# A graph network on one core: x copied into the first hop's table behind the table of places, by ScalarE, and no dense rounds beside the gathers of x

## What is computed

```
h = x
for k in 1..5:                       # layer 0: two such convolutions, 64 -> 128 -> 64
    msg = h[row] * norm[:, None]     # norm = dis[row] * edge_weight * dis[col]
    h   = segment_sum(msg, col, num_segments=100000)
    out = out + h @ W[k]
...
agg = segment_sum(x[src], dst) / count     # layer 1: means of neighbours, then attention of 4 heads
h   = agg @ W_sl + b_sl + x @ W_sr         # layers 2 and 3: such a mean, and attention again
```

## Time and profile before

| | us |
|---|---|
| timed runs, median of 3 | 11474.29 |
| lowest and highest of them | 11440.55, 11497.55 |
| profiled execution, first to last instruction (span) | 11533.1 |
| first gather of x | 18.5 |
| last gather of x | 875.8 |
| first gather of the first hop | 908.9 |

### The profile page before, as it was taken

One profiled execution on the slowest core, in us unless ns is written; L12 is line 12 of the kernel. 1 busy time (PEld: TensorE's weight loads), 2 busy tenths in 40 slices (PEclk: granted clock), 3 DMA queues, 4 the chain that ended last, 5 costly groups with the idle time before them and its releaser, 6 DMA issues. The chain is left out here.

```text
span 11533.1 us, 77998 instructions
## 1 busy us (share of the span) xinstructions
PE 6012.4 (52%) x19953; PEld 3133.7 (27%) x19953; DVE 5136.8 (45%) x14393; ACT 3452.3 (30%) x6468; POOL 6426.5 (56%) x6274
## 2 busy tenths in 40 slices
PE   1453545455454894535454440039778795530287
PEld 1442222222222442212122220013322463320154
DVE  1122333333333554445445446843434894440475
ACT  0002434334241332323233330013333573210143
POOL 6425556566555546556665666756555004657466
PEclk7556767777676996767677675559889897765698
DMA  5243322222223772222222222222233452222243
GB/s 155 55 61 89 89 73 88 79 74 80 66 85 103 214 215 77 79 64 82 76 77 85 65 75 65 76 56 63 65 62 63 138 187 69 65 56 51 78 136 109
DMA packets 1086306, 1021.95 MB, mean 89 GB/s; under 512 B 653551, under 2 KB 709245, under 8 KB 1073313
## 3 DMA queue, kind: packets, MB, share of 16 engines
q1 hardware_dynamic: 847422, 884.62, 24.7%
q0 software_dynamic: 200480, 130.29, 6.4%
q10 hardware_dynamic: 37955, 2.05, 0.4%
HBM read 494.44 MB, written 599.31 MB: 95 GB/s over the span
## 5 line engine op out<-in xcount | busy, mean ns | idle before, releaser
L762 POOL DMA_INDIRECT gathered<-u,place_of_source x1564 | 1625.6, 1039 | 955.9 <-issue 467.5
L762 POOL DMA_INDIRECT gathered<-hop,place_of_source x1564 | 1590.1, 1017 | 1015.5 <-DVE weighted L797 502.4
L811 DVE SCALAR_TENSOR_TENSOR sums<-sums,same_as_before,weighted 128x64 f32<-128x64 f32 x3510 | 987.3, 281 | 263.6 <-remote 109.8
L762 POOL DMA_INDIRECT gathered<-x,row_of_source x782 | 809.8, 1036 | 506.9 <-issue 245.1
L824 DVE SCALAR_TENSOR_TENSOR first_node_sum<-sums,ends_first,first_node_sum 128x64 f32<-128x64 f32 x2786 | 775.5, 278 | 136.2 <-remote 78.4
L695 DVE SCALAR_TENSOR_TENSOR dense_a<-dense_a 128x512 f32<-128x512 f32 x98 | 67.9, 693 | 1590.4 <-ACT dense_b L675 1251.2
L525 PE MATMUL bank<-dense_a,bd_gmean 128*128 128x512 f32 x196 | 195.9, 1102 | 939.3 <-ACT dense_out L516 581.9
L525 PE MATMUL bank<-dense_tmp,mean 128*128 128x512 f32 x980 | 553.5, 681 | 228.7 <-ACT dense_tmp L534 109.0
L762 POOL DMA_INDIRECT gathered<-in_x_dram,dst_index x392 | 393.1, 1003 | 470.6 <-DMA xc<-gathered 348.1
L2651 POOL DMA_INDIRECT out_dram<-lane_out,node_to_write x392 | 398.5, 1017 | 333.3 <-ACT lane_out L2570 224.1
L762 POOL DMA_INDIRECT gathered<-y,place_of_source x391 | 403.9, 1033 | 317.9 <-issue 116.0
(11 more groups left out here) (530 smaller groups left out, 14927.1 us busy)
## 6 DMA issues: line engine op xcount, KB each, us to landing
head_sums<-head_sums SPq DMA_DIRECT2D x98, 1024.0 KB
y<-conv_out SPq DMA_DIRECT2D x294, 256.0 KB
conv_out<-y SPq DMA_DIRECT2D x245, 256.0 KB
hop<-sums SPq DMA_DIRECT2D x196, 256.0 KB
turned<-rows_turned SPq DMA_DIRECT2D x196, 256.0 KB
cat<-turned SPq DMA_DIRECT2D x196, 256.0 KB
u<-conv_out SPq DMA_DIRECT2D x196, 256.0 KB
lane_raw<-x SPq DMA_DIRECT2D x196, 256.0 KB
```

What stands on the lines that cost most here:

```text
L762: return e.indirect_dma_start(out=into, out_offset=None, in_=tab, in_offset=bass.IndirectOffsetOnAxis(ap=index, axis=0), bounds_check=top, ...
L811: e.scalar_tensor_tensor(s[:, k, :], b, go[:, t:t + 1], m[:, k, :], ALU.mult, ALU.add).then_inc(st.summed.handle, 1)
```

## The change

- The copy of x leaves SP's list. ScalarE issues it: `x_in` for three blocks ahead of its part of the table, three more behind it, and then in a loop `x_out(b)` and `x_in(b + 4)` for all 98 blocks. There are `XB` = 6 buffers, three of them new, in `cat[1]`, which is free behind the table.
- All blocks get their places in the buffer before they are stored; `table_store` is gone, and so are the fills with "no place". Each store waits for its `table_place`.
- `weights_vector` becomes a list of steps. VectorE takes a step or so of it behind each `table_place`; the spreads of weights are issued at block 40 and waited for at block 50.
- The 16 groups of x gathers have no dense rounds any more: `EARLY` is 16, the slots of the hops share 16 rounds a lane, and those of the ups have one more round a lane than before.

The diff, cut to its core:

```diff
@@ -208,6 +208,7 @@
...
         SPREADS = 2 * (2 + 2 + 4)
+        SPREAD_BY = 50
...
@@ -338,23 +339,30 @@
...
         def weights_vector(e):
+            yield 0
...
             e.memset(t_m[:], 0.0).then_inc(chain.handle, 1)
+            yield 2
...
             e.memset(s_lin[:], 0.0).then_inc(chain.handle, 1)
+            yield 5
...
             e.tensor_copy(t_w3T[:].rearrange("p h d -> p (h d)"), PS[0][0:D, 0:W4]).then_inc(chain.handle, 1)
...
             e.tensor_copy(s_c, PS[3][0:D, 0:1]).then_inc(chain.handle, 1)
+            yield 12
...
             e.tensor_tensor(s_c, s_c, t_bb[0:D, 1:2], ALU.add).then_inc(chain.handle, 1)
+            yield SPREAD_BY
...
             e.tensor_reduce(t_v[:], t_bg[:], AX.X, ALU.add).then_inc(chain.handle, 1)
+            yield SPREAD_BY + 1
...
@@ -369,31 +377,41 @@
...
             e.tensor_tensor(wts["center"][:], wts["center"][:], ident[:], ALU.add).then_inc(chain.handle, 1)
+            yield SPREAD_BY + 2
...
             for i, w in enumerate(squares):
+                yield SPREAD_BY + 3 + 2 * i
...
                 e.tensor_copy(turned[:], PS[0][:, 0:P]).then_inc(chain.handle, 1)
...
             e.tensor_reduce(wts["v_lin"][0:2 * HEADS, :], t_b4[:, 0, :], AX.X, ALU.add).then_inc(chain.handle, 1)
+            yield SPREAD_BY + 29
...
             e.tensor_scalar(wts["v_lin"][0:2 * HEADS, :], wts["v_lin"][0:2 * HEADS, :], 0.2, None, ALU.mult).then_inc(chain.handle, 1)
+            yield 1 << 20
...
@@ -628,7 +646,7 @@
...
         if lo == 0:
-            yield W.n(0, 0)
+            yield -DENSE_STEPS
...
@@ -1006,7 +1024,10 @@
...
             xs = [a[:].rearrange("p k s d -> p (k s d)")[:, 0:K8 * XW].rearrange("p (k d) -> p k d", d=XW) for a in both]
+            XB = 6
             cat = [sb(ctx, f"cat{i}", [P, 2, 2, 512]) for i in range(2)]
+            xs += [cat[1][:].rearrange("p m a n -> p (m a n)")[:, i * K8 * XW:(i + 1) * K8 * XW].rearrange("p (k d) -> p k d", d=XW)
+                   for i in range(XB - len(both))]
...
@@ -1068,8 +1089,8 @@
...
             xc_got = [sem(f"xc_gathered{i}", 16 * K8 * n) for i, n in enumerate(in_slots(RING, lambda g: 1))]
-            xs_in = [sem(f"x_in{i}", 16 * len(range(i, DB, 3))) for i in range(3)]
-            xs_out = [sem(f"x_out{i}", 16 * len(range(i, DB, 3))) for i in range(3)]
+            xs_in = [sem(f"x_in{i}" if i < 3 else f"own_loaded{i - 3}", 16 * len(range(i, DB, XB))) for i in range(XB)]
+            xs_out = [sem(f"x_out{i}" if i < 3 else f"sums_stored{i - 3}", 16 * len(range(i, DB, XB))) for i in range(XB)]
...
@@ -1093,17 +1114,13 @@
...
             APART = DENSE_STEPS / DENSE_LANES
-            EARLY = 17
-            FREE = 16
-            PER_GROUP = 2
+            EARLY = 16
...
             LOADS_PER_GROUP = 6
-            STORES_PER_GROUP = 3
-            FREE_SHARE = 0.5
-            LATER = PER_GROUP * (NG - FREE)
-            placed_x = sem("shares_in_bank", DB - LATER)
+            SPREAD_AT, LINEAR_AT = 40, DB
+            placed_x = sem("shares_in_bank", DB)
             BUSY = NG - RING
-            SLOTS = len(hops) * BUSY + FREE_SHARE * FREE
+            SLOTS = len(hops) * BUSY
...
@@ -1112,8 +1129,7 @@
...
             def early(slot):
-                slots = FREE_SHARE * min(slot + 1, FREE) + busy_slots(slot + 1 - FREE)
-                return slots / SLOTS * (EARLY * DENSE_STEPS + 2 * APART)
+                return busy_slots(slot + 1) / SLOTS * (EARLY * DENSE_STEPS + 2 * APART)
...
@@ -1305,18 +1321,25 @@
...
 
-            def table_store(e, blocks):
-                e.wait_ge(*tv(6))
-                for b in blocks:
-                    at, n = node_rows(b)
-                    e.wait_ge(*xs_out[b % 3](16 * (b // 3 + 1)))
-                    e.dma_start(x66_rows[at:at + n * K8, 0:2].rearrange("(p k) v -> p k v", k=K8), table[0:n, b, :, :]
-                                ).then_inc(table_put.handle, 16)
+            def x_in(e, b):
+                i = b % XB
+                at, n = node_rows(b)
+                e.wait_ge(*xs_out[i](16 * (b // XB)))
+                e.dma_start(xs[i][0:n, :, 2:XW], x[at:at + n * K8, :].rearrange("(p k) d -> p k d", k=K8)
+                            ).then_inc(xs_in[i].handle, 16)
+            def x_out(e, b):
+                i = b % XB
+                at, n = node_rows(b)
+                e.wait_ge(*xs_in[i](16 * (b // XB + 1)))
+                e.wait_ge(*placed_x(b + 1))
+                e.dma_start(x66_rows[at:at + n * K8, :].rearrange("(p k) d -> p k d", k=K8), xs[i][0:n, :, :]
+                            ).then_inc(xs_out[i].handle, 16)
...
             def table_place(e, b):
-                i = b % 3
+                i = b % XB
                 n = node_rows(b)[1]
-                e.wait_ge(*xs_out[i](16 * (b // 3)))
+                e.wait_ge(*xs_out[i](16 * (b // XB)))
...
@@ -1491,9 +1514,8 @@
...
                     xc_gpsimd(e)
-                    e.wait_ge(*table_put(16 * LATER))
-                    for i in range(3):
-                        e.wait_ge(*xs_out[i](16 * len(range(i, DB, 3))))
+                    for i in range(XB):
+                        e.wait_ge(*xs_out[i](16 * len(range(i, DB, XB))))
...
@@ -1531,39 +1553,14 @@
...
 
-                    def x_in(b):
-                        i = b % 3
-                        at, n = node_rows(b)
-                        e.wait_ge(*xs_out[i](16 * (b // 3)))
-                        e.dma_start(xs[i][0:n, :, 2:XW], x[at:at + n * K8, :].rearrange("(p k) d -> p k d", k=K8)
-                                    ).then_inc(xs_in[i].handle, 16)
-                    def x_out(b):
-                        i = b % 3
-                        at, n = node_rows(b)
-                        e.wait_ge(*xs_in[i](16 * (b // 3 + 1)))
-                        if b >= LATER:
-                            e.wait_ge(*placed_x(b - LATER + 1))
-                        e.dma_start(x66_rows[at:at + n * K8, :].rearrange("(p k) d -> p k d", k=K8), xs[i][0:n, :, :]
-                                    ).then_inc(xs_out[i].handle, 16)
                     steps = early_steps(dense_sync, e)
-                    x_in(0)
                     for g in range(NG):
-                        for b in range(PER_GROUP * g, PER_GROUP * (g + 1)):
-                            if b + 1 < DB:
-                                x_in(b + 1)
-                            x_out(b)
...
                         deque(islice(weight_loads, LOADS_PER_GROUP), 0)
-                        if g > NG - FREE:
-                            table_store(e, range(LATER // 2 + STORES_PER_GROUP * (g - (NG - FREE) - 1),
-                                                 min(LATER, LATER // 2 + STORES_PER_GROUP * (g - (NG - FREE)))))
...
                         e.dma_start(columns(xc, g), flat(ring[i]).rearrange("p (k d) -> p k d", d=D)).then_inc(xc_put[i].handle, 16)
-                        steps.to(early(g - (NG - FREE) - 1))
                     deque(weight_loads, 0)
+                    steps.to(0)
...
@@ -1571,7 +1568,7 @@
...
                                 rows_keep(e, n, g - 2)
-                            steps.to(early(FREE + n * NG + g - 1))
+                            steps.to(early(n * NG + g - 1))
...
@@ -1656,13 +1653,11 @@
...
                     steps = early_steps(dense_tensor, e)
-                    for g in range(FREE):
-                        steps.to(early(g))
...
                                 hop_turn(e, st, n, g - 2)
-                            steps.to(early(FREE + n * NG + g - 0.2))
+                            steps.to(early(n * NG + g - 0.2))
...
@@ -1691,20 +1686,25 @@
...
                     planes_scalar(e)
+                    for b in range(len(both)):
+                        x_in(e, b)
                     table_scalar(e)
-                    weights_spread(e)
-                    table_store(e, range(0, LATER // 3))
+                    for b in range(len(both), XB):
+                        x_in(e, b)
+                    for b in range(DB):
+                        if b == SPREAD_AT:
+                            weights_spread(e)
+                        x_out(e, b)
+                        if b >= 2 and b + XB - 2 < DB:
+                            x_in(e, b + XB - 2)
                     weights_spread_linear(e)
-                    table_store(e, range(LATER // 3, LATER // 2))
...
                     steps = early_steps(dense_scalar, e)
-                    for g in range(FREE):
-                        steps.to(early(g))
...
                                 rows_move(e, n, g - 2)
-                            steps.to(early(FREE + n * NG + g))
+                            steps.to(early(n * NG + g))
...
@@ -1731,9 +1731,6 @@
...
                     e.memset(early_sum[0][:], 0.0)
-                    for i in range(3):
-                        e.memset(xs[i][:, :, 0].bitcast(I32), ABSENT)
-                        e.memset(xs[i][:, :, 1], 0.0)
...
@@ -1843,23 +1840,21 @@
...
```

(23 more changed lines are left out.)

3 lines of the change are left out of this document (added).

## The result

The changed kernel takes **11583.99 us** (median of 4 runs, 11533.68 to 11609.08), the kernel before in the same comparison 11485.92: **1.0078** of it, 95% interval 1.0046 to 1.0111. It is slower by 0.8%, some 53 to 127 us. The forecast was 11283, faster.

A forecast was written before the change was run, and what follows sets the result against it. The head was taken as bound by the table of places, late through a TensorE stall blamed on copies of x, then by the remaining copy. First hop -246, dense +50, hop start +5: -191 from 11474 gives 11283 us; range 11175 to 11570.

The forecast's parts named there:

- Copies out of the table's way: Head: without copies of x beside it, TensorE keeps its pace and the table is done at 410, 285 us earlier.
- My two counter-examples: TensorE at full pace beside gathers at 94.7 and after 909, taken as evidence that gathers alone don't cause the stall.
- SP stores xc without copies in between, so GpSimd ends near 535: Gathers of x: GpSimd no longer waits behind SP, and its end is covered by the copy.
- The copy behind the table: After the table: 98 blocks at 2.4 us, 235 us, plus 5 to fill and 10 for 16 spreads of weights.
- third rival: Copy crawls: the stall moves with the copies, 3.6 us a block, first hop at 766, 11386 us; chance 0.14.
- Dense rounds moved: Hops and ups: moving 45 steps a lane out of the gathers of x costs +50 us, between 25 and 108.
- Start of the first hop: First hop: TensorE may still be slow right behind the copies; +5 us, between 0 and 15.
- Nothing like it shows: First hop: after 909 the present trace was said to show no slow TensorE, so only 5 us were added.
- The second: Rival: the stall comes from gathers or something else that stays; table still at 695, 11560 us, slower; chance 0.08.
- The first rival: The stall belongs to the profiled execution alone; timed runs lack it, the change gives 11568 us, slower; chance 0.17.

The follow-up runs named there:

- pause_33: Changed kernel, but GpSimd waits for the table of places ahead of its group 33 of gathers of x; 1.0006 of the kernel before.
- pause_39: Changed kernel, but GpSimd waits for the table of places ahead of its group 39 of gathers of x; 1.0047 of the kernel before.
- fill_24: Changed kernel with a useless GpSimd instruction (0.47 us) behind each gather of x in the first 24 groups only; 0.9860 of the kernel before.
- before_fill: Kernel before, with a useless GpSimd instruction (0.47 us) behind each gather of x; 0.9769 of the kernel before.
- slow_gathers: Changed kernel with a useless GpSimd instruction (128x392 numbers) behind every gather of x; 0.9814 of the kernel before.
- dense_fill_half: Kernel before with a useless GpSimd instruction (128x196 numbers) behind each gather of x, plus the change's dense rounds moved; 0.9729 of the kernel before.
- fill_half_b: Repeat of fill_half, the whole change with the half-length useless instruction; 0.9743 of the kernel before.
- fill_half: Changed kernel with a useless GpSimd instruction (128x196 numbers) behind each gather of x; 0.9770 of the kernel before.
- half_rows: Changed kernel with every gather of x over 64 partitions instead of 128; 11583 us in one run, kernel before 11496.

## Why the prediction was wrong

**Copies out of the table's way (-285 us): this step failed.** It said that "I take the copies for its cause, with something that has to drain behind them". The table wasn't done at 410 but at 801, 106 us later than before. The rows for the other cause were on the page. From 390 to 460 TensorE was slow with nothing but gathers beside it, and I called that a draining of 80 us; the gathers had stopped at 438.8, 22 us before the stall ended, and I didn't put the two side by side. My two counter-examples didn't hold: at 94.7 the gathers had run for only 76 us, and "from 909 on 1004 matmuls run beside them without such gaps" was read from an average over 671 us, in which the trace has TensorE nearly still for stretches of some 50 us (above). An average row can't show that there are no gaps.

**The gain was also a new loss.** "SP stores xc without copies in between, so GpSimd ends near 535" was right (543.6), and it was the harm. SP's wait of 367.3 us had stopped the gathers and so freed TensorE. Without it the stall ran 107 us longer. That is how a kernel gets slower when a wait of 316 us goes: 801 - 695 = 106 us for the table, less what the copy gained. pause_33 and pause_39 show the link from the stop to the end of the stall.

**The copy behind the table: right, its cost too high.** 98 blocks took 172 us, 1.76 us each, where I took 2.4 with ends at 1.9 and 3.6: after 905 the DMA engines moved 312 GB/s, more than the 269 of the earlier trace rows. The 16 spreads took 10.6 us, 10 forecast. Beside gathers at full pace a block took 4.0 us (pause_33) and 6.4 (fill_24), more than the third rival's 3.6. So that rival describes something real, but not in this kernel. What I expected of fill_24, 2.74 us a block, was the mean of pause_33 over blocks beside gathers and behind them, and no price of either.

**Dense rounds moved (+50 us): mis-sized.** 12 us, with 25 to either side, and -14 us without the stall. I took a third of the way between 0.55 and 2.4 us a step. Even the low end, 25 us, is at the edge. That the steps fit into waits which the stages have anyway is my reading; no run shows it. The 3.1 us a group above GpSimd's pace, which I put down to the dense steps, can in part be the stall in the hops.

**Start of the first hop (+5 us): right in size, for a wrong reason.** Its first groups took 10.4 us each, as before. "Nothing like it shows" was wrong: TensorE slows behind 950 in the kernel before and behind 1020 in the changed one (no matmul from 1020 to 1040), so it cost nothing new.

**The sum.** First hop at 977.4 instead of 908.9, +68.5, and dense +12, is +81 us; the timed runs say +90 (53 to 127). For all kernels with several runs the start of the first hop carries most of the whole, within some 40 us: before_fill 232 us earlier and 268 us faster by the ratio, fill_24 148 and 162, slow_gathers 231 and 215.

**The rivals.** The second ("the stall comes from the gathers") was the case, with a chance of 0.08 and 11560 us, near the measured 11584. That it came so near is luck, since its errors nearly cancel: the table at 695 "still", which is 106 us too early, a copy 78 us too slow, and dense rounds 38 us too dear. The first rival, a stall of the profiled execution alone, fell. Each timed run comes with a span of its own, about 2 us under its time. Had they been free of the stall, the removal of it by the filler could not have brought the timed runs 215 to 300 us; so the stall is in all of them. By the Trainium skill ("NOTIFIC — the notification-queue block", "7.1 Overflow: three behaviours, one of which stalls the engine") the path of the records can hold back its producers; since every run here was recorded, none shows whether the stall would be there without records.

For the copy's issuer the Trainium skill ("DMA: Bandwidth & Descriptors", "Issuing engines are not separate DMA queues") said that ScalarE in place of SP brings nothing. dense_fill_half and fill_half_b differ in this and in the copy's place, and stand at 0.9729 and 0.9743. They don't speak against it, but they test it weakly: in both the gathers of x decide when the first hop starts.

## What to carry to other kernels

When an engine idles with nothing to wait for, list what every *other* engine does at the start and at the end of that stretch, and compare rates and not mere presence; the stall ended each time 20 to 27 us after one row, GpSimd's. Don't take an average over a long stretch as proof that there are no gaps in it; cut it into stretches of the length of the gap. Before a wait is taken away, ask what the waiting engine would do to the others if it ran free. And an engine off the critical path may be worth slowing: the kernel before with a useless instruction of 0.31 us behind each gather of x takes 0.974 of its time, and the restructuring that cost the work gained nothing beside it. Whether the same in the hops, over thousands of gathers, gains more is the next thing to try.

## What the runs showed of the hardware

- A row of GpSimd gathers at 1.30 us each slows TensorE's issue to one record in 2.8 us (one in about 0.25 otherwise), after some 20 us in fill_24 and some 100 us at the program's start. It ends 20 to 27 us after the gathers stop. With GpSimd's own pace at 1.34, 1.42 and 1.50 us a gather it is one in 1.4, one in 0.81, and no loss.
- The stall can reach GpSimd too: its gathers came every 1.40 us in place of 1.30 from 395 on in the changed kernel.
- Copies from ScalarE's queue slow down with it: 4.0 us a block beside gathers at 1.30 us and 1.83 behind them (pause_33), 1.96 and 1.98 beside gathers at 1.66 and 1.50 (slow_gathers, fill_half).
- In the stall, TensorE's signals reach VectorE up to 57 and 87 us after the matmul's end (118.3 to 175.1; 177.5 to 264.7), and most steps from one record to the next are multiples of about 0.7 us. That looks like a queue with a backlog, which signals or records share and which GpSimd's gathers fill. This is argued, not shown: what is queued there was not found, and what would tell it (a run without records, gathers without signals) wasn't tried.
- It goes by gather instructions, not by rows: with 64 partitions in place of 128 it was as long (half_rows, one run).
- Copies from SP's queue that keep the DMA engines 0.48 busy leave TensorE 99% busy, beside gathers at 1.66 us (before_fill).
